# The first node stage reads a second, transposed copy of x and leaves the transposes of x out

## The reference, cut to what matters

```
def _L0_gnn_ref(feat, W_neigh, b_neigh, src, dst):
    msgs = feat[src]
    neigh_sum = jax.ops.segment_sum(msgs, dst, num_segments=N)
    deg = jax.ops.segment_sum(jnp.ones(src.shape[0], feat.dtype), dst, num_segments=N)
    h_neigh = neigh_sum / jnp.maximum(deg, 1.0)[:, None]
    h = jnp.concatenate([feat, h_neigh], axis=1)
    return h @ W_neigh + b_neigh
...
x = _layernorm(x + _L0_gnn_ref(x, L0_gnn_W_neigh, L0_gnn_b_neigh, src, dst), axis=-1)
```

## Time and profile before

| what | value |
|---|---|
| median of three runs | 5701.69 us |
| the profiled execution, its own time | 5700.47 us |
| its span in the profile | 5698.6 us |
| TensorE matmul busy, whole span | 3631.1 us (64%) |
| VectorE, ScalarE, GpSimd busy | 3363.2, 2254.5, 3618.4 us |
| `node_sage`, first load to last store issue | 670.7 to 1013.9 us |
| data moved by DMA, whole span | 816.75 MB, mean 143 GB/s |

### The profile page before, as it was taken

One profiled execution on the slowest core, in us unless ns is written; L12 is line 12 of the kernel. 1 busy time (PEld: TensorE's weight loads), 2 busy tenths in 40 slices (PEclk: granted clock), 3 DMA queues, 4 the chain that ended last, 5 costly groups with the idle time before them and its releaser, 6 DMA issues. The chain is left out here.

```text
span 5698.6 us, 101401 instructions
## 1 busy us (share of the span) xinstructions
PE 3631.1 (64%) x21453; PEld 2571.3 (45%) x21454; DVE 3363.2 (59%) x13936; ACT 2254.5 (40%) x6392; POOL 3618.4 (63%) x4923
## 2 busy tenths in 40 slices
PE   4427799677788498969768888841005996200298
PEld 3427688676666244422246666631004775200033
DVE  6434477444478577777667777751614886334288
ACT  0015477566667233323257777720002442000055
POOL 2747566766635477716657777767575555757698
PEclk8759999899999799989889999965557998555599
DMA  1015577787889632201133333343115885511398
GB/s 28 1 39 161 168 238 227 213 242 217 234 256 280 212 112 52 53 8 36 32 103 119 121 125 120 122 134 76 31 41 194 291 291 189 135 36 41 115 342 301
DMA packets 551029, 816.75 MB, mean 143 GB/s; under 512 B 118566, under 2 KB 267629, under 8 KB 550466
## 3 DMA queue, kind: packets, MB, share of 16 engines
q1 hardware_dynamic: 354484, 506.90, 28.6%
q10 hardware_dynamic: 127152, 184.90, 9.1%
q0 software_dynamic: 69184, 122.90, 8.7%
HBM read 493.48 MB, written 329.46 MB: 144 GB/s over the span
## 5 line engine op out<-in xcount | busy, mean ns | idle before, releaser
L620 POOL DMA_INDIRECT agg_dst<-e_rows,e_put_i x392 | 390.8, 997 | 203.8 <-issue 118.9
L1867 POOL DMA_INDIRECT e_rows<-h,e_other_i x392 | 390.1, 995 | 149.3 <-issue 118.9
L1209 POOL TENSOR_TENSOR n_rstd<-n_rstd,minus_half 128x4 f32<-128x4 f32 x294 | 333.4, 1134 | 23.0
L689 POOL DMA_INDIRECT agg<-e_msg,e_put_i x196 | 194.9, 994 | 216.5 <-DVEq L718 165.2
L1222 ACT ACTIVATE n_o<-n_y_ps,n_shift,n_rstd 128x128 f32<-128x128 f32 x784 | 295.2, 464 | 13.2 <-POOL n_shift L1482 12.7
L2155 PE MATMUL n_y_ps<-n_w,n_gt 128*128 128x128 f32 x1568 | 270.4, 301 | 0.0
L364 POOL DMA_INDIRECT by_src<-s_pay_s,s_place_i x196 | 188.7, 963 | 113.9 <-issue 59.1
L1683 POOL DMA_INDIRECT lg_rows<-x,e_other_i x196 | 188.2, 960 | 109.9 <-issue 59.5
L937 PE MATMUL e1b_bank<-y_rows,e1b_hot 128*128 x1584 | 206.1, 291 | 81.1 <-ACT e1b_bank L1049 55.1
L895 POOL DMA_INDIRECT x_rows<-x,d_other_i x196 | 186.1, 949 | 112.5 <-issue 58.9
L937 PE MATMUL e1a_bank<-y_rows,e1a_hot 128*128 x1584 | 209.6, 294 | 73.8 <-ACT e1a_bank L1035 45.2
(11 more groups left out here) (513 smaller groups left out, 11899.0 us busy)
## 6 DMA issues: line engine op xcount, KB each, us to landing
n_ag<-agg_dst SPq DMA_DIRECT2D x294, 264.0 KB, 3.5
n_xs<-x SPq DMA_DIRECT2D x294, 256.0 KB, 3.4
h<-n_ho ACTq DMA_DIRECT2D x196, 264.0 KB, 3.4
n_hs<-h SPq DMA_DIRECT2D x196, 264.0 KB, 3.8
agg_dst<-e_ev SPq DMA_DIRECT2D x196, 132.0 KB
y<-n_o ACTq DMA_DIRECT2D x98, 264.0 KB, 3.1
e1a_fed<-y SPq DMA_DIRECT2D x196, 132.0 KB
m<-e1a_ev SPq DMA_DIRECT2D x196, 132.0 KB
```

Source lines behind the costliest of these rows:

```text
L620: pool.indirect_dma_start(out=agg, out_offset=bass.IndirectOffsetOnAxis(ap=e.put_i[:, c:c + 1], axis=0), in_=rows[:, c, :], in_offset=None ...
L689: pool.indirect_dma_start(out=agg, out_offset=bass.IndirectOffsetOnAxis(ap=e.put_i[:, c:c + 1], axis=0), in_=msg[:, g % SLOTS, k, 0:out_wi ...
L1209: st(pool.tensor_tensor(rstd, rstd, keep.minus_half[:, :], ALU.pow))
L1867: pool.indirect_dma_start(out=rows[:, c, :], out_offset=None, in_=h, in_offset=bass.IndirectOffsetOnAxis(ap=e.other_i[:, c:c + 1], axis=0))\
```

## The change

The host lays x out a second time, each block as [feature, group, partition], so that the turned x of a block is one contiguous run of 2048 bytes for each partition. `node_sage` loads that into `xt` and has neither `xs`, nor `xt_ps`, nor the transposes and the copy between them. The walk before it goes on reading the first copy. The load of `ag` comes first in SyncE's order and waits for `turned` as before; the load of `xt` comes after it and waits for `y_ready` of the block six before, since `xt` is now read by the product. TensorE's wait for x moves from `turn_over` to `product`.

```diff
+def block_turned(a, turn, s):
+    return a[turn * SLOT + s] if isinstance(turn, int) else a[bass.ds(turn * SLOT + s, 1)].squeeze(0)
...
-        xs, ag = ph.sb("xs", [P, SLOT, GB, D]), ph.sb("ag", [P, SLOT, GB, ROW])
+        ag = ph.sb("ag", [P, SLOT, GB, ROW])
...
-        xt_ps = [ph.ps(f"xt_ps{q}", [P, GB, P]) for q in range(BANKS)]
...
                 def load(turn, s, used):
                     sp.wait_ge(turned[s], used)
-                    sp.dma_start(xs[:, s], block_rows(x, turn, s)).then_inc(x_in[s], 16)
                     sp.dma_start(ag[:, s], block_rows(agg, turn, s)).then_inc(ag_in[s], 16)
+                    sp.wait_ge(y_ready[s], used)
+                    sp.dma_start(xt[:, s], block_turned(x_turned, turn, s)).then_inc(x_in[s], 16)
...
                 def turn_over(turn, s):
-                    done(pe, x_in, turn, s, 16)
                     done(pe, meaned, turn, s)
-                    bank_free(pe, moved, turn, s, 2, BANKS)
-                    for g in range(GB):
-                        pe.transpose(xt_ps[s % BANKS][:, g, :], xs[:, s, g, :], keep.ident[:, :])
+                    bank_free(pe, moved, turn, s, 1, BANKS)
                     for g in range(GB):
                         ins = pe.transpose(at_ps[s % BANKS][:, g, :], ag[:, s, g, 0:D], keep.ident[:, :])
                     ins.then_inc(turned[s], 1)
 
                 def product(turn, s):
-                    done(pe, moved, turn, s, 2)
-
+                    done(pe, x_in, turn, s, 16)
+                    done(pe, moved, turn, s)
                     bank_free(pe, x1_ready, turn, s, 1, YBANKS)
...
                     free(act, y_ready, turn, s)
-                    act.activation(xt[:, s], xt_ps[s % BANKS][:, :, :], ACT.Copy).then_inc(moved[s], 1)
                     act.activation(at[:, s], at_ps[s % BANKS][:, :, :], ACT.Copy).then_inc(moved[s], 1)
...
+    rows = padded(inputs["x"], NPAD, 0)
+    x, x_turned = take("x", rows), take("x_turned", rows.reshape(NB, P, GB, D).transpose(0, 3, 2, 1))
```

More of the change, by code:

```diff
@@ L1257, in pipeline, with node_sage @@
         steps(turn, True)
-def node_sage(nc, keep, x, agg, w, bias, y1):
+def node_sage(nc, keep, x_turned, agg, w, bias, y1):
     with Phase(nc, "n0", freed="turned added stored y_ready x1_ready sums_ready meaned inverted") as ph:
@@ L2588, in _, with gnn @@
                 act.wait_ge(stored, 16)
-def gnn(nc, x, src, dst, attr, sage, gcn, gat2, gat, out):
+def gnn(nc, x, x_turned, src, dst, attr, sage, gcn, gat2, gat, out):
     def dram(name, shape):
@@ L2619, in gnn @@
                 walk(nc, keep, "e0", on_dst, rows, x, ROW, agg_dst, FromZero(ROW))
-            node_sage(nc, keep, x, agg_dst, sage["W"], sage["b"], y1)
+            node_sage(nc, keep, x_turned, agg_dst, sage["W"], sage["b"], y1)
             with nc.sbuf_tensor("y_rows", [P, J, ROW], F32) as rows:
@@ L2654, in layer @@
         return w
-    x = take("x", padded(inputs["x"], NPAD, 0))
+    rows = padded(inputs["x"], NPAD, 0)
+    x, x_turned = take("x", rows), take("x_turned", rows.reshape(NB, P, GB, D).transpose(0, 3, 2, 1))
     src, dst = (take(n, padded(inputs[n], EPAD, NPAD - 1)) for n in ("src", "dst"))
@@ L2666 @@
     out = nc.dram_tensor("out", (NPAD, D), F32, kind="ExternalOutput").ap()
-    gnn(nc, x, src, dst, attr, {"W": sage["W_neigh"], "b": sage["b_neigh"]}, gcn, gat2, gat, out)
+    gnn(nc, x, x_turned, src, dst, attr, {"W": sage["W_neigh"], "b": sage["b_neigh"]}, gcn, gat2, gat, out)
     r = run_bass_kernel_spmd(nc, [arrays], core_ids=[0])
```

## The result

Four runs of the changed kernel have a median of 5643.9 us (5634.8 to 5649.0), four of the kernel before 5699.5; the ratio is 0.9895 with an interval of 0.988 to 0.991, so 51 to 68 us are gone, 56 by the medians. 5652 was forecast. The profiled execution took 5640.2 us.

What follows compares the result with a forecast made beforehand. ScalarE was taken to bound the changed phase, just ahead of TensorE. 48.2 us of rate plus 1.5 at the start, off 5700.5, gave 5650.8, and 1.2 for the median made 5652.0 us; range 5641 to 5668.

Steps and rivals of the forecast that it cites:

- ScalarE as the bound: Changed phase's block loop: ScalarE sets the pace, TensorE 0.13 us behind; step falls from 3.31 to 2.81 us.
- TensorE's own steps: Changed phase's loop: TensorE alone needs 3.18 us a block before, 2.74 after four transposes go.
- VectorE's wait: Changed phase's loop: VectorE's wait for the product falls from 0.65 to about 0.15 us.
- Rate: Changed phase's 97 steps: 92 lose 0.50 us and 5 lose 0.44, 48.2 us in all.
- Start: Start of the changed phase: earlier `ag` issue and four fewer cold transposes save 1.5 us, between 0 and 2.5.
- Sum: Whole program: 48.2 + 1.5 = 49.7 us off the profiled execution's 5700.5.
- SyncE's new wait and the later loads: Load order in the changed phase: waiting for `y_ready` and issuing `ag` and turned x later cost nothing.
- Transfers: Changed phase's DMA: rate rises from 237 to about 280 GB/s, share from 0.74 to 0.87, cost taken as 0.
- The high end of 12 us: Changed phase's load waits at 0.13 us a block; rival of DMA or a three-engine race, 5664 us, chance 0.11.
- TensorE's clock: Changed phase: clock stays at 1.00, its 2.4 GHz level, cost zero; rival of a lower clock, 5822 us, slower chance 0.04.
- The rule by occupancy: Changed phase: highest occupancy makes TensorE the bound, only its 0.44 us returns; TensorE's-pace rival 5657.5 us, chance 0.13.
- All phases behind keep their lengths: Sign for the unedited phases after the changed one: no change in their lengths.

Runs made afterwards that it cites:

- pe_extra: Changed kernel with TensorE transposing the means a second time into banks nothing reads: ratio 0.9958, changed phase 335.4 us.
- store_sp: Changed kernel with the store issued by SyncE instead of ScalarE: ratio 0.9897 to the kernel before, changed phase 293.5 us.
- second pair: Kernel before and changed kernel, both run again unchanged on other chips: changed phase 357.7 and 308.4 us.
- Experiment 5: Two more profiles of each unchanged kernel: `node_gatv2`, first to last load, 811.7 and 809.3 us before, 808.1 and 811.7 us changed.
- act_extra: Changed kernel with ScalarE copying the turned means a second time into a tile nothing reads: ratio 0.9996, changed phase 352.2 us.
- b_again: Kernel before, run again unchanged on another chip: ratio 0.9997, changed phase 357.7 us.
- a_again: Changed kernel, run again unchanged: ratio 0.9911 to the kernel before, changed phase 308.4 us.

## Why the prediction was right or wrong

- ScalarE as the bound, 0.13 us before TensorE: right. Step 2.81 forecast, 2.78 to 2.87 measured; 3.2 at a turn's end, 3.16 measured; mean with the branches 2.87 forecast, 2.87 measured. Adding the copy alone gave nearly the old time back, 352 of 356 us.
- TensorE's own steps of 3.18 and 2.74: right, 3.17 in `pe_extra` and 2.73 in `store_sp`. VectorE's wait: 0.15 forecast, 0.20 measured.
- Rate 48.2 us: 47.5 measured. Start 1.5 us: the first copy of ScalarE comes 18.8 us after the first weight load instead of 20.5, so 1.7. Sum 49.7 against 49.2, and 49.3 on the second pair.
- SyncE's new wait and the later loads at nothing: right, no wait of 700 to 940 us names a transfer.
- Transfers: 280 GB/s and 0.87 forecast, 279 and 0.90 measured. The high end of 12 us for their waits was mis-sized: with 369 GB/s the whole stretch lost 1.7. The row that it rested on, showed a late load in another stage, not a limit of the transfers.
- TensorE's clock in the steady part of the phase: 1.00, right.
- The rule by occupancy (the Trainium skill, Perfetto Trace Analysis, "Identifying the Most-Contended Engine"): after the change weight loads are at 195 of 240 us and ScalarE at 182, so by that rule TensorE is the bound once more. `store_sp` took 0.34 us of issue from ScalarE and nothing from TensorE, and the phase fell by 15 us: the measurement decides, ScalarE was the bound, with a quarter of its time shown idle.
- The failing step is "All phases behind keep their lengths", a term put at nothing without a spread. By the medians the gain is 6 us above the sum, and the ratio times the median before is 5640, under the range's low end of 5641. In the two profiles 11 us of the gain lie outside of the changed phase: `node_gatv2` is 11.9 shorter and the edge phase before it 8.2 longer, without an edit, and the other parts together some 7 shorter. Experiment 5 shows the larger of these varying by 14 us within one kernel. The range held a part of one median's 6 us and no term for the unedited phases on either side of a comparison. The mechanism was right and its sum came within 0.5 us of the changed phase; whether the 6 us on top are chance or in part a consequence of the change stays open.
- On the chips of the experiments the phases behind did not keep their lengths either, and there it repeats. The two walks between the changed phase and the second layer's stage took 1018.9 to 1022.1 us in four profiles with the instructions of before and 1017.7 in `act_extra`, but 1006.7 to 1011.6 in the seven others. The difference lies in the second walk alone, here the first and last start of its loads in `b_again`, `act_extra` and `a_again`:

```profile
L1027 SPq DMA_DIRECT2D e1b_fed<-m x196: 337/338/1393, 1810.9 to 2309.3; - x196
L1027 SPq DMA_DIRECT2D e1b_fed<-m x196: 17/338/717, 1803.2 to 2300.3; - x196
L1027 SPq DMA_DIRECT2D e1b_fed<-m x196: 17/338/1393, 1765.6 to 2252.4; - x196
```

- These are 498, 497 and 487 us; the other profiles have 496 to 499 where ScalarE makes two copies in the changed phase and 486 to 488 where it makes one, while the first walk's loads take 489 to 493 in all twelve. On the first chip both walks together took 582.0 and 581.3 (the second was 6 us shorter after the change, the first 4 longer). So it does not explain the recorded result, but it is why ratios there are nearer to 0.991 than the 0.993 that 49 us of 6970 would be. It goes with ScalarE's extra copy, which is not in that walk; its mechanism wasn't tried and stays open.

## What to carry to other kernels

Write one engine's step out from start to start, with its DMA issues and its own semaphore round trips: the bound may be an engine that the profile shows as three quarters busy, and a bracket that names another engine may hold its own issue time. When two engines are within 4% of each other, as here, an edit is worth its full size only if it relieves both. Give the phases that are not edited a spread of their own, on both sides of the comparison. When the bound moved from ScalarE to TensorE, ScalarE's branches of each turn were covered as well; count with the mean that includes them.

## What the runs showed that was not expected

- Transfers of 1040 KB a block ran at 369 GB/s with a busy share of 1.02, their landing going from 3.1 and 3.9 us to 3.9 and 4.9, and 1.7 us were lost, though 0.94 at 281 GB/s had looked like a full queue.
- One kernel, two executions: 823.4 and 809.3 us in a phase of equal work, with 132 and 101 us at TensorE's lower clock.
- A walk that nobody edited is 10 us shorter on three chips when ScalarE makes one copy fewer in a phase that ends 500 us before it.
